# A two-layer graph network: where x is loaded, where constants are made, how lookups compare, and the last round of layer 1

## The reference

```python
# layer 0
out_deg = maximum(segment_sum(ones, src), 1)
in_cnt = segment_sum(ones, dst)
t1 = x @ W1
msg = t1[src] + x[src] * x[dst] @ W2
msg = msg / (sqrt(out_deg[src]) * sqrt(out_deg[dst]))[:, None]
embed = where(in_cnt > 0, t1 + segment_sum(msg, dst), 0) + b
embed = leaky_relu(embed, 0.01)
x = layernorm(x + embed / maximum(norm(embed), 1e-12))
# layer 1
xt = x @ W.T + b
out = segment_sum(xt[src], dst) / (segment_sum(ones, dst) + 1)
x = layernorm(x + out)
```

## Time and profile before

| | |
|---|---|
| median of 3 runs | 4010.15 us (4009.8 to 4021.47) |
| the profiled execution | 4012.56 us, span 4010.7 us |
| PE busy | 3025.4 us, 75% |
| POOL busy | 2994.5 us, 75% |
| DVE busy | 1981.0 us, 49% |
| ACT busy | 473.9 us, 12% |
| chain that ended last | POOL 71%, issue 25%, PE 1% |

### The profile page before, as it was taken

The page is one execution under the profiler, slowest core; times in us unless marked ns, Lnnn a source line. Parts: engine busy times, 40 slices in busy tenths (PEclk is TensorE's granted clock), DMA queues, the critical chain, the costliest instruction groups (busy, mean ns, idle before and its releaser), DMA issues.

```text
span 4010.7 us, 43591 instructions
## 1 busy us (share of the span) xinstructions
PE 3025.4 (75%) x10770; PEld 1838.6 (46%) x10770; DVE 1981.0 (49%) x3850; ACT 473.9 (12%) x1459; POOL 2994.5 (75%) x3147
## 2 busy tenths in 40 slices
PE   4443677777777777777777878888887888878877
PEld 3432455555555555555543434334443443333433
DVE  9998555656666565666533232323232323232323
ACT  5553200000000000000000000000000000000000
POOL 4777777777777777777767777777777777777776
PEclk5555788888888888888877676776667666676677
DMA  9779444444444444544434443444443434444443
GB/s 272 210 210 318 146 143 143 143 144 143 143 143 143 143 145 144 151 142 143 135 105 120 115 120 115 120 115 119 115 120 115 120 115 120 115 120 115 120 115 106
DMA packets 314688, 564.23 MB, mean 141 GB/s; under 512 B 62726, under 2 KB 214628, under 8 KB 314660
## 3 DMA queue, kind: packets, MB, share of 16 engines
q0 software_dynamic: 150048, 409.93, 36.0%
q10 hardware_dynamic: 77438, 75.21, 5.9%
q1 hardware_dynamic: 87174, 78.78, 5.9%
HBM read 487.95 MB, written 75.72 MB: 141 GB/s over the span
## 4 chain that ended last, share of the span: by engine, by line
POOL 71%; issue 25%; SPq 1%; POOLq 1%; PE 1%; DVE 0%; DMA 0%; DVEq 0%; ACT 0%; ACTq 0%
POOL ring L476 64%; POOL ring L488 6%; SPq L350 1%; POOL ring L480 1%; PE banks L1217 0%; POOLq L517 0%; DVEq L710 0%; POOLq L471 0%; PE banks L1254 0%; DMA early_rows<-ring 0%; POOLq L472 0%; PE banks L1206 0%; DMA ring<-scaled_x,idx 0%; DMA ring<-zeros_x,idx 0%; SPq L339 0%
## 5 line engine op out<-in xcount | busy, mean ns | idle before, releaser
L1254 PE MATMUL banks<-ring,hot_space 128*128 128x257 f32 x6252 | 2453.2, 519 | 664.3 <-DMA ring<-zeros_x,idx 324.4
L1254 PEld LDWEIGHTS banks<-ring,hot_space 128*128 128x128 f32 x6252 | 1306.4, 241 | 1724.6 <-DMA ring<-zeros_x,idx 1099.2
L476 POOL DMA_INDIRECT ring<-zeros_x,idx x1563 | 1487.7, 952 | 486.6 <-issue 475.6
L476 POOL DMA_INDIRECT ring<-scaled_x,idx x1249 | 1201.7, 962 | 380.5 <-issue 380.5
L906 DVE SCALAR_TENSOR_TENSOR big<-banks,here_mask,big 128x257 f32 x784 | 343.0, 479 | 1521.4 <-PE banks L1254 1521.2
L874 DVE TENSOR_TENSOR hot_space<-banks,dst_rel 128x1024 f32<-128x1024 f32 x395 | 483.6, 1224 | 227.9 <-issue 201.9
L488 POOL DMA_INDIRECT ring<-in_x,src_col x276 | 262.7, 952 | 118.3 <-issue 83.5
L611 ACT COPY idx<-src_col 128x8 int32 (+1 forms) x392 | 77.2, 197 | 2182.1 <-PE banks L1254 2134.7
L1122 PE MATMUL banks<-hot_space 128*128 128x98 bf16 x1280 | 119.0, 282 | 175.2 <-DVE hot_space L717 175.2
L1122 PEld LDWEIGHTS banks<-hot_space 128*128 128x128 bf16 x1280 | 102.0, 141 | 192.3 <-DVE hot_space L717 183.5
L1206 PE MATMUL banks<-ident,halves 128*128 128x128 f32 x588 | 131.0, 375 | 76.8 <-DVE halves L918 71.4
(11 more groups left out here) (150 smaller groups left out, 1210.5 us busy)
## 6 DMA issues: line engine op xcount, KB each, us to landing
early_rows<-ring SPq DMA_DIRECT2D x282, 128.0 KB, 3.0
ring<-early_rows ACTq DMA_DIRECT2D x47, 768.0 KB, 6.5
ring<-zeros_x,idx POOLq DMA_INDIRECT x1563, 2.8
ring<-scaled_x,idx POOLq DMA_INDIRECT x1249, 2.8
zeros_x<-out_t SPq DMA_DIRECT2D x98, 128.0 KB
big<-in_x SPq DMA_DIRECT2D x1, 12416.0 KB
result<-out_t SPq DMA_DIRECT2D x97, 128.0 KB
x_t<-zeros_x ACTq DMA_DIRECT2D x96, 128.0 KB, 2.3
```

The source lines that it names most:

```text
L476: g.indirect_dma_start(ring[:, u, 0:D], None, (table[0] if layer == 0 else zeros_x1) if rows is None else rows, bass.IndirectOffsetOnAxis( ...
L1254: last = nc.tensor.matmul(group_sum(k), dst_hot[:, k % HOTS, u - k * GT, :], ring[:, u, 0:DW], start=u == tiles[0], stop=u == tiles[-1])
```

## The change

x is loaded in 14 parts of 7 node tiles, each issued by SP behind every 16th store of a staging slot; only its last 84 rows are still loaded ahead. POOL makes the identity first (with a semaphore of its own, which PE waits for), issues the six early gathers, and makes the other constants behind them. The 276 staging gathers then wait for the edges in columns and as floats, no longer for the first indices and `step_digits_made`; the raw gathers wait for these. `find_r` compares with `lane_row`, which is in PSUM. The last round of layer 1 takes the order of layer 0's last round, ACT's roots included, and builds no one-hots after its first group. The waits for stored rows in `finish_sums` stand directly ahead of writing `out_t`.

```diff
+X_LOADS = 14
+X_LOAD_EVERY = 16
...
-            sp.wait_ge(x_padded, 1)
-            x_rows = x[0:(NW - 1) * P, :].rearrange("(w p) f -> p w f", p=P)
-            sp.dma_start(x_all[:, 0:NW - 1, :], x_rows).then_inc(x_loaded, 16)
-            sp.dma_start(x_all[0:LAST_ROWS, NW - 1, :], x[(NW - 1) * P:NODES, :]).then_inc(x_loaded, 16)
...
+            def load_some_x(c):
+
+                first, end = c * NW // X_LOADS, min((c + 1) * NW // X_LOADS, NW - 1)
+                sp.dma_start(x_all[:, first:end, :],
+                             x[first * P:end * P, :].rearrange("(w p) f -> p w f", p=P)).then_inc(x_loaded, 16)
+
+            sp.wait_ge(x_padded, 1)
+            sp.dma_start(x_all[0:LAST_ROWS, NW - 1, :], x[(NW - 1) * P:NODES, :]).then_inc(x_loaded, 16)
             for n in range(len(SPILLS)):
                 store_spill(n)
+                if n % X_LOAD_EVERY == X_LOAD_EVERY - 1 and n // X_LOAD_EVERY < X_LOADS:
+                    load_some_x(n // X_LOAD_EVERY)
...
+            nc.gpsimd.memset(ident[:, :], 0.0).then_inc(ident_made, 1)
+            g.wait_ge(ident_made, 1)
             nc.gpsimd.affine_select(out=ident[:, :], in_=ident[:, :], compare_op=ALU.not_equal, fill=1.0, base=0,
-                                    pattern=[[-1, P]], channel_multiplier=1).then_inc(consts_made, 1)
+                                    pattern=[[-1, P]], channel_multiplier=1).then_inc(ident_made, 1)
...
             for n in range(EARLY):
                 gather_spill(n)
+            nc.gpsimd.iota(count_to[:, :, :], pattern=[[1, P], [0, PAIR]], base=0, channel_multiplier=0,
+                           allow_small_or_imprecise_dtypes=True).then_inc(consts_made, 1)
...
+            g.wait_ge(edges_in_cols, 1)
+            g.wait_ge(edges_float, 2)
+            for n in range(EARLY, len(SPILLS)):
+                gather_spill(n)
             g.wait_ge(idx_ready, 4)
             g.wait_ge(step_digits_made, 1)
-            for n in range(EARLY, len(SPILLS)):
-                gather_spill(n)
             for u in range(RAW_FIRST):
                 gather_raw(u)
...
-            act.wait_ge(x_loaded, 32)
+            act.wait_ge(x_loaded, 16 * (X_LOADS + 1))
...
-                        with act.Fori(1, ROUNDS) as i:
+                        with act.Fori(1, ROUNDS - 1) as i:
                             round_(layer, i, True)
+                        round_(layer, ROUNDS - 1, True, roots_first=True)
...
                 shape = [P, count, HI]
-                nc.vector.tensor_tensor(space, src_hi[:, bass.ds(first_tile, count)].unsqueeze(2).to_broadcast(shape),
-                                        count_to[:, 0:HI, 0].unsqueeze(1).to_broadcast(shape), ALU.is_equal)
+                nc.vector.tensor_tensor(space, lane_row[:, 0:HI].unsqueeze(1).to_broadcast(shape),
+                                        src_hi[:, bass.ds(first_tile, count)].unsqueeze(2).to_broadcast(shape), ALU.is_equal)
...
             def finish_sums(layer, m, sums):
 
-                for s in range(2):
-                    v.wait_ge(stored[s], 16 * (node_no(layer, m) + 1))
                 if layer == 0:
...
                     for s in range(2):
+                        v.wait_ge(stored[s], 16 * (node_no(1, m) + 1))
                         nc.vector.scalar_tensor_tensor(out_t[s][:, :], project[s], scal[:, 2 + s:3 + s], e[s][:, :],
...
-                    group_hot(first_tile, (k + AHEAD) % HOTS,
-                              raw=layer == 0 and isinstance(i, int) and first_tile < RAW,
-                              early=layer == 0 and finish and not last and k == 0)
-                    if last and layer == 0 and k == LAST_K + 1:
+                    if not (last and layer == 1 and k > 0):
+                        group_hot(first_tile, (k + AHEAD) % HOTS,
+                                  raw=layer == 0 and isinstance(i, int) and first_tile < RAW,
+                                  early=layer == 0 and finish and not last and k == 0)
+                    if last and k == LAST_K + 1:
                         finish_sums(layer, i - 1, acc[:, bass.ds(2 * i - 2, 2), :])
                         moments(layer, i - 1)
                     add_group(layer, i, k, block)
...
-                        if last and layer == 0:
+                        if last:
                             if k == LAST_K + 1:
                                 norm(layer, i - 1)
...
-            pe.wait_ge(consts_made, 17)
+            pe.wait_ge(ident_made, 2)
...
             turn_edges(1)
+            pe.wait_ge(consts_made, 15)
```

More of the change, by code:

```diff
@@ L208, in gnn @@
         candidates = banks[:, 4:6, 0:HALF_TILES * HI]
+        ident_made = sem("ident_made")
         consts_made = sem("consts_made")
@@ L438, in _ @@
         def _(g):
[L439 to L458, removed]
@@ L459, in _ @@
-            nc.gpsimd.affine_select(out=ident[:, :], in_=ident[:, :], compare_op=ALU.not_equal, fill=1.0, base=0,
-                                    pattern=[[-1, P]], channel_multiplier=1).then_inc(consts_made, 1)
[L461 to L467, removed]
+            nc.gpsimd.memset(ident[:, :], 0.0).then_inc(ident_made, 1)
@@ L494, in _ @@
                 gather_spill(n)
+            nc.gpsimd.iota(count_to[:, :, :], pattern=[[1, P], [0, PAIR]], base=0, channel_multiplier=0,
+                           allow_small_or_imprecise_dtypes=True).then_inc(consts_made, 1)
+            nc.gpsimd.iota(lane[:, :], pattern=[[0, 1]], base=0, channel_multiplier=1,
+                           allow_small_or_imprecise_dtypes=True).then_inc(consts_made, 1)
+            nc.gpsimd.iota(floor_i[:, :], pattern=[[2 * P, GPB // GR], [0, GR]], base=-2 * P,
+                           channel_multiplier=2 * P * (GPB // GR)).then_inc(consts_made, 1)
@@ new lines, in _ @@
+            nc.gpsimd.iota(floor_late[:, :, :], pattern=[[2 * P, GPB // GR], [0, GR - LAST_K - 1]], base=0,
+                           channel_multiplier=2 * P * (GPB // GR)).then_inc(consts_made, 1)
+            nc.gpsimd.iota(dump_row[:, :], pattern=[[0, 1]], base=DUMP, channel_multiplier=1,
+                           allow_small_or_imprecise_dtypes=True).then_inc(consts_made, 1)
+            nc.gpsimd.memset(lower[:, :], 1.0).then_inc(consts_made, 1)
+            nc.gpsimd.memset(ones[:, :], 1.0).then_inc(consts_made, 1)
@@ new lines, in _ @@
+            nc.gpsimd.memset(zeros[:, :], 0.0).then_inc(consts_made, 1)
+            nc.gpsimd.memset(epsilon[:, :], 1e-5).then_inc(consts_made, 1)
+            nc.gpsimd.iota(columns[:, :], pattern=[[1, P]], base=0, channel_multiplier=0,
+                           allow_small_or_imprecise_dtypes=True).then_inc(consts_made, 1)
+            nc.gpsimd.memset(between[:, :], 0.0).then_inc(consts_made, 1)
+            g.wait_ge(consts_made, 11)
+            nc.gpsimd.affine_select(out=lower[:, :], in_=lower[:, :], compare_op=ALU.is_gt, fill=0.0, base=0,
+                                    pattern=[[-1, P]], channel_multiplier=1).then_inc(consts_made, 1)
@@ new lines, in _ @@
+            for n, (value, offset) in enumerate(((0.25, 0), (-0.25, 1), (0.25, 1 - P))):
+                g.wait_ge(consts_made, 12 + n)
+                nc.gpsimd.affine_select(out=between[:, :], in_=between[:, :], compare_op=ALU.not_equal, fill=value,
+                                        base=offset, pattern=[[-1, P]], channel_multiplier=1).then_inc(consts_made, 1)
+            g.wait_ge(edges_in_cols, 1)
+            g.wait_ge(edges_float, 2)
+            for n in range(EARLY, len(SPILLS)):
+                gather_spill(n)
@@ L550, in _ @@
                 nc.scalar.copy((src_col[:, 0:TILES], dst_col[:, :])[n], cols).then_inc(edges_in_cols, 1)
-            act.wait_ge(consts_made, 17)
+            act.wait_ge(consts_made, 15)
             act.drain()
@@ L748, in _ @@
             last.then_inc(step_digits_made, 1)
-            v.wait_ge(consts_made, 17)
+            v.wait_ge(consts_made, 15)
             v.wait_ge(edges_in_cols, 2)
@@ L779, in _ @@
             ordered()
-            v.wait_ge(x_loaded, 32)
+            v.wait_ge(x_loaded, 16 * (X_LOADS + 1))
             for c, (first, end) in enumerate(X_CHUNKS):
@@ L936, in finish_sums @@
                     for s in range(2):
+                        v.wait_ge(stored[s], 16 * (m + 1))
                         nc.vector.tensor_tensor_reduce(out=out_t[s][:, :], in0=e[s][:, :], in1=e[s][:, :], scale=1.0,
```

## The result

| | before | changed |
|---|---|---|
| median of 4 executions | 4009.98 us (4008.59 to 4021.47) | 3977.68 us (3975.44 to 3978.37) |
| span of the profiled one | 4010.7 us | 3976.2 us |

The account below looks back on a forecast made before the run. POOL's gathers at 1.25 us each, plus its stalls, were taken as the bound. Start 23.7, lookup 6 and last round 2 sum to 31.7 us: 3980.9 profiled, 3978.5 as median; range 3969 to 3990.

Parts of the forecast that it names:

- the start: Time up to layer 0's second quarter of round 1: 23.7 us gained, bounds 13 and 28.
- the lookup: Layer 0's comparison L862 with an input in PSUM no longer stretches gathers: 6 us gained, bounds 2 and 8.
- the later waits: Waits for stored rows moved later in finish_sums: over before the products were there, so worth nothing.
- POOL as the bound, and the release of the slots: POOL's gathers, 1.25 us each, bound the kernel; x in parts removes its 29.5 us wait for a staging slot.
- F: Time at which POOL ends the raw gathers and the first quarter of round 1 may start: 405.3.
- The next wait is ACT's clearing: POOL, ready for round 1's second quarter at 415.3, waits about 8 us for indices ACT refills after clearing the sums.
- D': New time at which the cleared sums release DVE to add group 0: 412.1, against 420.7 before.
- the table 9.5 us sooner: ACT's scaled-table store finishes 9.5 us sooner, since staging stores end at about 375 and free DMA bandwidth.
- rival A: Table lands no sooner because its queue sets the rate: D' 421.6, gain 22 us, time 3988; chance 0.16.
- The step from D' to the second quarter: From DVE's release to the first gather of round 1's second quarter: 11.6 us, so the wait ends at 423.7.
- rival B: L862 is not what holds layer 0's gathers, which stretch as before: gain 25.7 us, time 3984.5; chance 0.10.
- Layer 1's last round: Statistics go before group 2, so the last sums are added sooner: 2.0 us gained, bounds 1 and 4.

Follow-up runs that it names:

- e6: Changed kernel with DVE instead of ACT clearing chunks 5 to 7 of the sums; 3968.29 us.
- e8: Changed kernel with DVE clearing chunks 5 to 7, ACT's zero-row stores issued at the start, and round 0's turn_lo ahead of the late one-hots; 3964.53 us.
- e9: Changed kernel with x in 2 parts instead of 14, behind the 16th and 32nd store; 3984.57 us, one execution of four far off.
- e3: Kernel before with only the waits for stored rows moved behind the projected products; 4015.32 us, where the kernel before took 4019.27.
- e5: Changed kernel with the waits for stored rows back at the head of finish_sums; 3983.11 us.
- e10: Changed kernel with x in one part behind the 16th store instead of 14 parts; 3994.24 us.
- e1: Kernel before with only x loaded in 14 parts; 4002.29 us, where the kernel before took 4019.27.
- e2: Kernel before with only find_r's comparison reading lane_row in PSUM; 4011.28 us, where the kernel before took 4019.27.
- e4: Changed kernel with the old comparison of src_hi with count_to, both in SBUF; 3993.44 us, where the kernel before took 4019.27.

## Why the prediction was right, and where it was not

The mechanisms at the start, in the lookup and in the last round are as forecast. The nearness of the sum is not earned: the start gave 5.5 us less than its term, the lookup 2.7 more, and the later waits some 4 to 5 where nothing was claimed.

- **POOL as the bound, and the release of the slots: right.** F = 405.3 was 405.0.
- **The next wait is ACT's clearing: right**, shown by e6 and e8. Its place was early by 5 us: D' was given as 412.1 and is 416.93. The early edges cost 0.5 instead of 0.9, so the mis-sized term is "the table 9.5 us sooner"; it is 4.3. It has two parts. The table's last store, which took 24.9 us to land, now lands 17.5 us after its issue at 380.28, at 397.8 instead of 404.1: 6.3 us sooner, or 6.8 without the delay, where 10.8 was worked out. And ACT goes on when its issues are done, not when they land: its last one ends at 393.92 instead of 397.71, 3.8 sooner. The forecast passed the gain in landing on to ACT in full.

```profile
scaled_x<-big ACTq DMA_DIRECT2D x1, 1024.0 KB, 17.5
```

  For the landing, the forecast let the table have the staging stores' share from 375 on. The packets and megabytes of each queue (q10 is ACT's, q1 is SP's, q0 POOL's), before in 375 to 385, then changed in 375 to 385 and in 385 to 395:

```profile
q10 hardware_dynamic: 1818, 1.85, 53.1%
...
q1 hardware_dynamic: 989, 0.90, 26.0%
```
```profile
q10 hardware_dynamic: 2004, 2.03, 60.4%
...
q1 hardware_dynamic: 720, 0.66, 19.0%
...
q10 hardware_dynamic: 2802, 2.84, 80.0%
...
q0 software_dynamic: 401, 1.09, 27.3%
```

  SP's last store is issued by 374.0, but 0.66 MB of stores are moved after 375: while the engines were full its queue had fallen behind. The table goes at 203 GB/s until 385, against 185 before, and at 284 only from there, as the forecast had it for 375 (279). The measured D' lies half way between the forecast and rival A (421.6). In e9, with later staging stores, the clearing is later too.
- **The step from D' to the second quarter** was taken as 11.6 from a case in which POOL was not waiting. The indices come at D' + 11.3, as read, but a POOL that waits starts 0.98 us after the start of ACT's copy, not 0.3.
- **The lookup: right in mechanism, 6 for 8.7.** The 26 gathers across L862 cost 7.4 us by the trace, not 7.0. The 47 that lie beside an L862 without being long, which spoke for rival B, speak against it: they start before it or in its last 0.12 us. The holds at L916 and L918 shrank too, from 8.5 to 4.9 us, and those at L934 and L937 grew from 2.2 to 4.4: probably gathers that L862 no longer pushes back fall otherwise on them.
- **The later waits: priced at nothing, worth about 4 to 5 us** (e3, e5). The step that failed is "in the other rounds POOL covers them". POOL covers a late DVE, but where DVE's operations fall against POOL's gathers sets how long those last.
- **Layer 1's last round: right.** 2.0 forecast, 2.7 read, of which 0.7 is the clock during the last products. Tails of the runs with the new order are 12.97 to 14.47 us, with the old one 16.18 to 16.76.
- **The row of 41.88 us was misread.** It is L350, the load of the last 84 rows; the 12.4 MB are L349, issued just ahead in 0.43 us. What is held is the DMA behind a large one, as e10 shows. The 3.0 us a part was still high enough a price: after a part the next store's issue took at most 2.36 us, and no slot was waited for.

## What to carry to other kernels

Once a stall on the bounding engine is to go, work out the next release on another engine before claiming the whole stall; here 29.5 us and 5.3 us gave 18, and shortening the next one (e6 to e8) gave another 13. When a stream on shared DMA engines ends early, credit the others from the time its queue is empty, not from its last issue. The time at which a store lands and the time at which its issuer is free are two numbers; take the one that the next step waits for. Here a gather's issue was held when it started while DVE ran an operation with two inputs in SBUF: moving one input to PSUM took the hold away, and starting such an operation sooner shortened it.

## What was not expected of the hardware

- A tenth or two of a microsecond in DVE's order was worth 4 us, through the 0.08 us by which each of some 45 gathers is held.
- L985, which scales one tensor in SBUF by two columns of scalars, holds gathers too: 25 of the 33 that start inside it before. Two tensors in SBUF are not the only case.
- A gather's issue does not take the same time in all executions. Those that nothing holds take 945 ns in the mean before, in the changed kernel, in e3 and in e5 to e10, and 948 in the profiled executions of e1, e2 and e4; the gap to the next one is 305 ns in all. Over 3126 gathers 3 ns are 9 us. That is about the difference between the kernel before on the two chips (4019.27 and 4010.16). e3 is from the same chip as e1, e2 and e4; its profiled execution, with the 945 ns, took 4006.72, and the median of its executions is 4015.32. This has nothing to do with a change, and its cause stays open.
